# A DLRM tower taken in pairs of units inside a running pipeline, with the last two units cut into parts

## The chip, the cores and the metric

The program runs on one core of one Trainium2 chip. The time is the device time of one execution in microseconds (us); of a kernel that was run several times the median is given. Engines are named as the profile names them: PE is TensorE (PEld its weight loads), DVE is VectorE, ACT is ScalarE, POOL is GpSimd, SP is SyncE, which here only issues DMAs.

## The reference

512 samples, 16 embedding tables of width 256, three compressed-interaction layers, and a small MLP tower.

```python
e = stack([tbl_f[ids[:, f]] for f in range(16)], axis=1)        # 512 x 16 x 256
xk = e
for i in range(3):
    z = einsum('bfe,bge->bfge', e, xk).reshape(B, 256, 256)
    z = relu(einsum('bcl,oc->bol', swapaxes(z, 1, 2), Ws[i]) + bs[i][None, :, None])
    z = sum(z, axis=-1)                                         # 512 x 16
    outs.append(z)
    xk = broadcast_to(z[:, :, None], (B, F, E))
h = concatenate([outs, dense_ctx], axis=1)                      # 512 x 64
h = maximum(h @ W_top1 + b_top1, 0)                             # 64 -> 512
h = maximum(h @ W_top2 + b_top2, 0)                             # 512 -> 256
y = h @ W_top3                                                  # 256 -> 1
```

Everything is float32. The first layer needs all pair products of the 16 features. In layers 2 and 3 `xk` is constant along E, so one layer is a 16x16 table of outer products per sample, a bias and ReLU, and a sum.

## The kernel before

**Units and steps.** The batch is cut into NU = 16 units of 32 samples. A unit passes through the engines over several steps, and step n works on several units at once:

- POOL gathers unit n+2 with four indirect DMAs (`gather`), and forms part of unit n's pair products (`multiply`, `pool_rows(n)` of the 8 rows of the largest rectangle: 4 in most steps, 0 in step 0, 6 in steps 14 and 15).
- PE transposes unit n+1 (`transpose`, into PSUM tile `T`), contracts the products of unit n-1 with the first layer's weights in two halves (`contract`, into `Y`), spreads z over rows for stage n-2 (`spread_rows`, into `ZB`), and projects unit n for layers 2 and 3 (`layer_u`, into `YD`).
- ACT copies `T` to `XT` (`fill`), squares (`square`), copies `YD` to `U` (`read_u`), sums layer 1 (`sum_y`), and sums the outer products of stage n-2, eight blocks of 256 with bias, ReLU and an accumulator (`sum_prod`).
- DVE forms the rest of the pair products (`products`), masks z (`spread_z`, into `zx`) and forms the outer products of stage n-2 (`outer`, into `prod`). A stage s has up to two halves (s, 0) and (s, 1): layer 2 of unit s and layer 3 of unit s-1.

Each engine runs its own fixed list of instructions, in the order of the program text. Semaphores tie the lists together; nothing is reordered by a planner. A wait on an engine holds up all that stands behind it on that engine.

**The tower** runs over three chunks of units, (0, 6), (6, 12), (12, 16). For each chunk PE first moves the sums into rows of `H` by small matmuls with `sel_sb` (`select`), then runs hidden layer 1 (4 matmuls), hidden layer 2 (8 matmuls) and the output (2 matmuls). `MLP_STEPS` places chunk 0 in steps 11 to 15, after the transposes and ahead of `layer_u`; chunks 1 and 2 stand mostly behind the last step. A float32 matmul is two passes on PE, each with its own weight load, and the profile counts the passes.

**The tail** handles stages 14, 15 and 16 after the last contraction. DVE and ACT share its sums (`TAIL_SHARE`), DVE takes over some of the tower's evacuations (`DVE_PIECES`), and stage 16's z goes to `Y` (`zb_last`).

**Unit 0** has all its products on DVE; `dve_products` is raised once, after both halves, so `contract(0, ., 0)` waits for the whole unit. PE transposes units 0 and 1 first, then projects unit 0, then contracts it.

## Time and profile before

| | us |
|---|---|
| median of 3 runs | 172.34 (171.52 to 172.9) |
| the profiled execution | 171.46 |
| its span in the trace | 169.6 |
| PE busy | 137.1 (81%) |
| DVE busy | 144.9 (85%) |
| ACT busy | 126.3 (74%) |
| POOL busy | 121.0 (71%) |

The span is the profiled execution's time without 1.86 us around it. The profiled execution is 0.5% under the median. Busy shares are averages over a filling phase, a regular phase of equal steps (about 30 to 130 us) and a tail (about 140 us to the end); each phase has its own limit.

### The profile page before, as it was taken

What the parts mean: (1) busy time and instruction counts of PE and PEld (TensorE: products, weight loads), DVE (VectorE), ACT (ScalarE), POOL (GpSimd) and SP (SyncE); (2) the same over time, 40 slices, a digit from 0 to 9 for tenths busy, and PEclk for the clock granted to TensorE, in tenths of its full rate; (3) what the DMA queues carried; (4) which work ended last, traced back from release to release, by engine and by line L of the source; (5) the groups of instructions that cost most, each with busy time, mean ns of one, the idle gap of its engine ahead of it and who ended that gap; (6) DMA issues with size and microseconds to landing.
All of it is one profiled execution on the core that took longest, in us unless ns stands there. A gap on an engine that the chain in (4) does not pass through costs nothing.

```text
span 169.6 us, 6453 instructions
## 1 busy us (share of the span) xinstructions
PE 137.1 (81%) x2728; PEld 92.4 (54%) x2728; DVE 144.9 (85%) x136; ACT 126.3 (74%) x441; POOL 121.0 (71%) x84
## 2 busy tenths in 40 slices
PE   0045998988887878787879797999898999993995
PEld 0024665746464646464646464757474876763963
DVE  3169986999999999999999999999999998198330
ACT  3020465586979797979797979798999998977461
POOL 1777989898888888888888888989797995000000
PEclk9999999999999999999999999999999999999599
DMA  2343653131313030303030303031313100000000
GB/s 56 94 123 97 190 151 97 30 98 37 93 33 95 25 101 12 112 9 117 2 114 10 103 20 103 24 99 35 96 32 97 31 4 4 6 0 2 4 0 0
DMA packets 5273, 9.98 MB, mean 59 GB/s; under 512 B 2179, under 2 KB 2947, under 8 KB 5252
## 3 DMA queue, kind: packets, MB, share of 16 engines
q0 software_dynamic: 3072, 8.39, 17.2%
q1 hardware_dynamic: 2036, 1.29, 2.8%
q8 instruction: 14, 0.23, 0.6%
q14 instruction: 7, 0.06, 0.1%
q10 hardware_dynamic: 144, 0.00, 0.0%
HBM read 9.68 MB, written 0.00 MB: 57 GB/s over the span
## 4 chain that ended last, share of the span: by engine, by line
PE 46%; DVE 19%; ACT 18%; issue 8%; POOL 4%; DMA 3%; DVEq 1%; ACTq 0%
PE Y L627 25%; DVE PR L311 13%; ACT prod L387 8%; ACT XT L357 7%; PE T L592 5%; POOL X L329 4%; PE T L688 4%; PE ZB L648 4%; DVE prod L503 3%; PE Y L633 2%; ACT Y L378 2%; PE YD L670 2%; DMA X<-in_table,idx 2%; PE YD L688 2%; PE YD L604 1%
## 5 line engine op out<-in xcount | busy, mean ns | idle before, releaser
L311 DVE TENSOR_TENSOR PR<-T,XT 128x1024 f32<-128x1024 f32 (+2 forms) x72 | 101.1, 1450 | 7.0 <-ACT XT L357 6.9
L627 PE MATMUL Y<-PR,w_sb 128*32 128x272 f32 x1024 | 66.0, 399 | 13.0 <-DVE PR L311 12.6
L329 POOL DMA_INDIRECT X<-in_table,idx x64 | 61.2, 956 | 20.7 <-issue 16.1
L387 ACT ACTIVATE prod<-prod,bias_sb 128x256 f32<-128x256 f32 x122 | 60.1, 498 | 4.2 <-DVE prod L503 4.2
L311 POOL TENSOR_TENSOR PR<-XT 128x2048 f32<-128x2048 f32 (+2 forms) x16 | 59.7, 3734 | 0.3
L627 PEld LDWEIGHTS Y<-PR,w_sb 128*32 128x32 f32 x1024 | 31.1, 110 | 35.7 <-issue 12.1
L503 DVE TENSOR_TENSOR prod<-U,ZB 128x2048 f32<-128x2048 f32 (+1 forms) x18 | 35.6, 1982 | 3.4 <-PE ZB L648 3.3
L378 ACT ACTIVATE Y<-Y,bias 128x136 f32<-128x136 f32 x64 | 21.5, 336 | 14.2 <-PE Y L633 14.2
L592 PE MATMUL T<-ident_sb,X 128*128 128x128 f32 x128 | 21.7, 314 | 12.3 <-DMA X<-in_table,idx 12.3
L357 ACT ACTIVATE XT<-T 128x1024 f32<-128x1024 f32 (+1 forms) x17 | 16.6, 974 | 18.1 <-PE T L592 13.2
L592 PEld LDWEIGHTS T<-ident_sb,X 128*128 128x128 f32 x128 | 17.5, 211 | 14.0 <-issue 9.9
L387 ACT ACTIVATION_READ_ACCUMULATOR prod<-prod,bias_sb 128x1 f32 x122 | 23.3, 191 | 0.0
L363 ACT ACTIVATE PR<-XT 128x1024 f32<-128x1024 f32 x16 | 16.9, 1057 | 0.0
L378 ACT ACTIVATION_READ_ACCUMULATOR Y<-Y,bias 128x1 f32 x64 | 12.7, 198 | 0.0
L633 PEld LDWEIGHTS Y<-minus_half,b0row_sb 1*32 1x32 f32 x256 | 4.9, 102 | 14.0 <-issue 14.0
L604 PE MATMUL YD<-XT,w1l_sb 128*32 128x64 f32 x512 | 11.1, 228 | 0.0
L604 PE MATMUL YD<-XT,w2l_sb 128*32 128x64 f32 x512 | 10.7, 225 | 0.0
L604 PEld LDWEIGHTS YD<-XT,w1l_sb 128*32 128x32 f32 x512 | 8.4, 113 | 2.2 <-issue 1.0
L648 PE MATMUL ZB<-zx,spread_sb 128*128 128x128 f32 (+1 forms) x32 | 7.7, 322 | 2.2 <-DVE zx L489 2.2
L604 PEld LDWEIGHTS YD<-XT,w2l_sb 128*32 128x32 f32 x512 | 8.9, 114 | 0.0
L633 PE MATMUL Y<-minus_half,b0row_sb 1*32 1x32 f32 x256 | 8.4, 202 | 0.0
L648 PEld LDWEIGHTS ZB<-zx,spread_sb 128*128 128x128 f32 x32 | 4.8, 188 | 3.7 <-issue 2.0
(48 smaller groups left out, 69.3 us busy)
## 6 DMA issues: line engine op xcount, KB each, us to landing
X<-in_table,idx POOLq DMA_INDIRECT x64, 2.8
w_sb<-in_w SPq DMA_DIRECT2D x1, 512.0 KB
w_sb<-in_w SPq DMA_DIRECT2D x1, 224.0 KB
sel_sb<-in_sel SPq DMA_DIRECT2D x1, 128.0 KB
ident_sb<-in_ident SPq DMA_DIRECT2D x1, 64.0 KB, 2.1
w1l_sb<-in_w1l SPq DMA_DIRECT2D x1, 64.0 KB
w2l_sb<-in_w2l SPq DMA_DIRECT2D x1, 64.0 KB
w_sb<-in_w SPq DMA_DIRECT2D x1, 64.0 KB
```

Of the source, the lines that this page charges most:

```text
L311: return eng.tensor_tensor(pr, x0.broadcast_to(shape), x1.broadcast_to(shape), ALU.mult)
L329: pool.indirect_dma_start(out=X[:, n % NV, g, :], out_offset=None, in_=table, in_offset=bass.IndirectOffsetOnAxis(ap=idx[:, NT * n + g:NT ...
L357: act.activation(x, t, ACT.Copy).then_inc(xt_ready, len(qs))
L363: act.activation(pr[:, :, PAIRS:COLS], x.rearrange("q (n f) -> q n f", f=F), ACT.Square, scale=ROOT_HALF).then_inc(squared, 1)
L378: last = act.activation(y, y, ACT.Relu, bias=bias2[:], scale=2.0, accum_out=zz[:, n, k:k + 1])
L387: last = act.activation(q, q, ACT.Relu, bias=bias_sb[:, l + 1:l + 2], accum_out=to)
L503: dve.tensor_tensor(prod[:, s % 2, b0:b1, :, :], stage_u(s)[:, b0:b1, :].rearrange("q b (f x) -> q b f x", x=1) .broadcast_to([P, nb, F, F ...
L592: last = pe.transpose(T[:, v, h, c, :], X[:, v, 2 * h:2 * h + 2, :].rearrange("q g (e c) -> q c (g e)", c=NC) [:, c, :], ident_sb[:])
L604: last = pe.matmul(YD[TR * j:TR * j + TR, SB * F * l:SB * F * (l + 1)], w[:, c, :], XT[:, v, :, c, CB * F * j:CB * F * (j + 1)], start=c = ...
L627: pe.matmul(Y[TR * j:TR * j + TR, h, 0:YC], w0_sb[:, c, :], PR[:, v, h, c, CB * j:CB * (j + 1), :].rearrange("q b s -> q (b s)"), start=c ...
L633: last = pe.matmul(out_d[:, :, PAIRS:COLS], b0row_sb[:], minus_half[:].rearrange("q (b f) -> q b f", b=CB), start=False, stop=True)
L648: pe.matmul(zb_of[:, b0:b1, :], spread_sb[:], zx[:, b0:b1, :], start=True, stop=True)\
```

## The change

1. **Start.** Unit 0's products are handed over by halves. PE contracts half 0 before it transposes the second half of unit 1, and half 1 after `layer_u` of unit 0. `keep_busy` puts 10, 8 and 4 matmuls without use of their results between the first waits.
2. **Tower in pairs.** The chunks are (0, 2), (2, 4), (4, 6), (6, 8), (8, 10), (10, 12), (12, 16). From step 5 on, every odd-numbered step of the unit counter selects chunk k and runs hidden layer 2 of chunk k-1; the step after it runs the output of chunk k-1 and hidden layer 1 of chunk k. They stand where `tower_step` stood, between the transposes and `layer_u`, and the loop of steps now covers 7 to 14. `h1` is read by one activation instead of four; the first bias is a row of `w1_sb`.
3. **Copies.** The sums of a pair are first copied by SP, with three DMAs in SBUF, into `pair`, from which PE selects. SP waits for the ACT sums of half (2k+2, 1) and for the previous select.
4. **Last two units.** Stages 14 and 15 are spread and multiplied in parts (`PIECES`), and their spreads stand inside `contract`; `prod` has three buffers instead of two; POOL takes 4 rows in step 14 and 8 in step 15. `layer_u` of unit 15 is done layer by layer.
5. **Folds.** Halves (13, 1) and (14, 1) are folded by POOL from 256 to 64 columns and summed by one DVE reduction each.

The core of the diff (`...` marks what is left out):

```diff
-POOL_ROWS = {0: 0, NU - 2: 6, NU - 1: 6}
-LOOP = range(3, 11)
-CHUNKS = [(0, 6), (6, 12), (12, 16)]
+POOL_ROWS = {0: 0, NU - 1: 8}
+ACT_SHARE = {(NU - 2, 0): 2, (NU - 1, 1): 2, (NU, 1): 2, (NU - 3, 1): 0, (NU - 2, 1): 0}
+FOLDS = [(NU - 3, 1), (NU - 2, 1)]
+PIECES = [(NU - 2, 0), (NU - 2, 1), (NU - 1, 0), (NU - 1, 1), (NU, None)]
+PIECE_BLOCKS = [(0, SB), (SB, 2 * SB), (0, CB), (CB, 2 * SB), (SB, 2 * SB)]
+CHUNKS = [(0, 2), (2, 4), (4, 6), (6, 8), (8, 10), (10, 12), (12, 16)]
+FIRST = 5
+PW = 2 * UB
+LOOP = range(FIRST + 2, NU - 1)
...
+            for k in range(LAST - 1):
+                sp.wait_ge(z0_ready, 2 * CHUNKS[k][1])
+                wait_sums(sp, (CHUNKS[k][1], 1))
+                wait(sp, selected, k)
+                for l, src in enumerate(sums_of(*CHUNKS[k])):
+                    sp.dma_start(pair[:, l, :, :], src).then_inc(paired, 16)
...
+                pool.tensor_tensor(q[:, :, 0:P], q[:, :, 0:P], q[:, :, P:2 * P], ALU.add)\
+                    .then_inc(pool_step, 1)
...
+            def tower_select(n, k):
+                pe.wait_ge(u_read, n)
...
+                if first >= 1:
+                    pe.wait_ge(h1_ready, k)
+                if not isinstance(k, int) or in_flow(k):
+                    pe.wait_ge(paired, 16 * 3 * (k + 1))
+                    select_chunk(selected_psum(0), [pair[:, l, :, :] for l in range(3)])
+                if first >= 1:
+                    for c in range(HC2):
+                        second_hidden(k - 1, c)
+            def tower_hidden(n, k):
+                pe.wait_ge(u_read, n)
+                pe.wait_ge(h_ready, k + 1)
+                wait(pe, h2_ready, HC2 * k)
+                if not isinstance(k, int) or k >= 1:
+                    outputs(k - 1)
+                first_hidden(k, ...)
...
             transpose(0, 0, 0)
+            keep_busy(ZB[:, 2 * P:3 * P], 8)
             pe.wait_ge(consts_in, 16 * 5)
             pe.wait_ge(minus_half_ready, 1)
-            transpose(1, 1, 0)
+            pe.matmul(mask_g_ps, ...).then_inc(mask_ready, 1)
+            transpose(1, 1, 0, (0,))
+            keep_busy(ZB[:, 2 * P:3 * P], 4)
+            contract(0, 0, 0)
+            transpose(1, 1, 0, (1,))
+            layer_u(0, 0)
+            contract(0, 0, 1)
+            transpose(2, 0, 1)
+            layer_u(1, 1)
...
+            with nc.tensor.Fori(1, len(LOOP) // NV + 1) as i:
+                n = NV * i + FIRST
+                step(n, 1, i + FIRST // NV)
+                tower_select(n, i)
+                layer_u(n, 1)
+                step(n + 1, 0, i + FIRST // NV + 1)
+                tower_hidden(n + 1, i)
+                layer_u(n + 1, 0)
```

What PE runs in one pair of regular steps, before (the body of its loop, two steps; `T` transposes, `Y` the contractions, `ZB` the spread, `YD<-XT` the projection `layer_u`):

```order
L627 MATMUL Y<-PR,w_sb 32x272 x16
L633 MATMUL Y<-minus_half,b0row_sb 32x2x16 x4
L592 MATMUL T<-ident_sb,X 128x128 x8
L599 ISA
L604 MATMUL YD<-XT,w1l_sb 32x64 x16
L604 MATMUL YD<-XT,w2l_sb 32x64 x16
```

Now, from the transposes of the select step to its projection, and the same place of the step after it:

```order
L693 MATMUL T<-ident_sb,X 128x128 x8
L793 ISA
L751 MATMUL YD<-pair,sel_sb 32x4x2 x24
L772 MATMUL YD<-h,w_sb 128x64 x8
L700 REGISTER_ALU
L706 MATMUL YD<-XT,w1l_sb 32x64 x16
```

```order
L693 MATMUL T<-ident_sb,X 128x128 x8
L779 MATMUL YD<-h,w_sb 1x64 x2
L765 ISA
L765 MATMUL YD<-H,w_sb 128x64 x4
L700 REGISTER_ALU
L706 MATMUL YD<-XT,w1l_sb 32x64 x16
```

Each pair of steps has gained 24 small and 14 tower matmuls; before, steps 3 to 10 held none of them. The end of PE's list, before, behind the last contraction:

```order
L684 MATMUL T<-H,w_sb 128x192 x4
L648 MATMUL ZB<-zx,spread_sb 128x128
L670 MATMUL YD<-zz,sel_sb 32x8x2 x8
L670 MATMUL YD<-zz,sel_sb 32x6x2 x8
L670 MATMUL YD<-z,sel_sb 32x4x2 x8
L688 MATMUL T<-h,w_sb 128x192 x4
L648 MATMUL Y<-zx,spread_sb 128x64
L688 MATMUL T<-h,w_sb 128x192 x4
```

and now:

```order
L706 MATMUL T<-XT,w2l_sb 32x64 x16
L743 MATMUL ZB<-zx,spread_sb 128x96
L772 MATMUL YD<-h,w_sb 128x64 x8
L743 MATMUL T<-zx,spread_sb 128x64
L751 MATMUL YD<-zz,sel_sb 32x4x2 x16
L751 MATMUL YD<-z,sel_sb 32x4x2 x8
```

The spread of stage 16 (128x64) stood behind a hidden layer of 192 columns; it now stands behind one of 64.

## Rows read from the trace of the kernel before

**Rows 1.** Busy time of each engine in two stretches (us, count), then PE's clock, DMA.

```profile
80.00:90.00 10.00, 8.50 (x183) 5.38 (x186) 10.00 (x7) 9.05 (x33) 8.90 (x6) 1.00 0.22 66
...
150.00:160.00 10.00, 7.06 (x71) 6.53 (x72) 6.35 (x16) 6.95 (x28) 0.00 (x0) 0.85 0.01 2
```

**Rows 2.** Timeline, DVE, one regular step: start, duration, what, count, [idle before <- releaser].

```profile
79.13 0.27 DVE L489 TENSOR_TENSOR zx<-zz,ZB 128x128 f32<-128x128 f32 x1
...
87.65 0.28 DVE L489 TENSOR_TENSOR zx<-zz,ZB 128x128 f32<-128x128 f32 x1
```

**Rows 3.** Timeline, PE, one regular step and the start of the next.

```profile
85.88 2.04 PE L627 MATMUL Y<-PR,w_sb 128*32 128x272 f32 x32 [1.50 <-DVE PR L311]
...
90.63 1.23 PE L592 MATMUL T<-ident_sb,X 128*128 128x128 f32 x8
...
91.80 0.65 PE L604 MATMUL YD<-XT,w1l_sb 128*32 128x64 f32 x32
...
92.27 0.63 PE L604 MATMUL YD<-XT,w2l_sb 128*32 128x64 f32 x32
```

**Rows 4.** Timeline, PE: loads under 16 columns; step 11 with select; unit 15's transposes.

```profile
21.87 0.30 PEld L709 LDWEIGHTS ZB<-mask_g_sb,ident_sb 128*128 128x128 f32 x2
...
107.60 1.23 PE L592 MATMUL T<-ident_sb,X 128*128 128x128 f32 x8
...
109.98 0.25 PE L604 MATMUL YD<-XT,w1l_sb 128*32 128x64 f32 x2
...
132.94 1.23 PE L592 MATMUL T<-ident_sb,X 128*128 128x128 f32 x8
```

**Rows 5.** Timeline, ACT, the same regular step.

```profile
83.43 1.02 ACT L357 ACTIVATE XT<-T 128x1024 f32<-128x1024 f32 x1 [0.36 <-issue]
...
84.35 0.50 ACT L387 ACTIVATE prod<-prod,bias_sb 128x256 f32<-128x256 f32 x1
...
88.28 0.26 ACT L369 ACTIVATE U<-YD 128x128 f32<-128x128 f32 x1
...
90.77 0.35 ACT L378 ACTIVATE Y<-Y,bias 128x136 f32<-128x136 f32 x1 [0.57 <-PE Y L633]
```

**Rows 6.** DMA issues: what, queue, kind, count, size, median us from issue to landing.

```profile
X<-in_table,idx POOLq DMA_INDIRECT x64, 2.8
...
bias_sb<-in_bias SPq DMA_DIRECT2D x1, 1.5 KB, 1.8
```

**Rows 7.** Timeline, SP's issue of a DMA, and POOL around its last gather.

```profile
1.66 0.42 SPq L283 DMA_DIRECT2D bias_sb<-in_bias  x1
...
130.18 0.94 POOL L329 DMA_INDIRECT X<-in_table,idx  x1 [0.30 <-issue]
131.14 8.38 POOL L311 TENSOR_TENSOR PR<-XT 128x3072 f32<-128x3072 f32 x2
```

**Rows 8.** Timeline, the start: DVE's and PE's first work, DVE's second wait.

```profile
9.96 14.73 DVE L311 TENSOR_TENSOR PR<-T,XT 128x1024 f32<-128x1024 f32 x12 [4.82 <-ACT XT L357]
...
18.96 2.79 PE L627 MATMUL Y<-PR,w_sb 128*32 128x272 f32 x32 [0.37 <-ACT PR L363]
...
26.81 2.29 DVE L311 TENSOR_TENSOR PR<-T,XT 128x2048 f32<-128x2048 f32 x1 [2.11 <-ACT XT L357]
```

**Rows 9.** Timeline, the tail, from the last contraction to the last activation.

```profile
149.73 0.26 PE L633 MATMUL Y<-minus_half,b0row_sb 1*32 1x32 f32 x8
...
154.93 0.22 DVE L489 TENSOR_TENSOR zx<-zz,ZB 128x64 f32<-128x64 f32 x1
...
156.53 2.44 PE L688 MATMUL T<-h,w_sb 128*128 128x192 f32 x8
...
158.77 0.53 PE L648 MATMUL Y<-zx,spread_sb 128*128 128x64 f32 x2
...
159.53 1.22 DVE L503 TENSOR_TENSOR prod<-U,Y 128x1024 f32<-128x1024 f32 x1 [3.21 <-PE Y L648]
...
167.71 0.27 ACT L395 ACTIVATE y_sb<-Y 1x128 f32<-1x128 f32 x1 [1.35 <-PE Y L693]
```

More of the change, by code:

```diff
@@ L19 @@
 NV = 2
+NPR = 3
 EH = 64
@@ L697, in _, with select_chunk, first_hidden @@
-            pe.wait_ge(ident_in, 16)
+            def select_chunk(to, layers):
+                for l, src in enumerate(layers):
+                    last = select(to, l, src)
+                last.then_inc(selected, 1)
+            def first_hidden(k, cols):
+                w = 0 if not isinstance(k, int) else k
+                per = HC1 // len(hidden1_psum(w))
+                for c in range(HC1):
+                    pe.matmul(hidden1_psum(w)[c // per][:, c % per, :], w1_sb[:, c * P:(c + 1) * P],
+                              H[:, cols], start=True, stop=True).then_inc(hidden1, 1)
@@ new lines, in second_hidden, with outputs @@
+            def second_hidden(k, c):
+                w = 0 if not isinstance(k, int) else k
+                for q in range(HC1):
+                    last = pe.matmul(hidden2_psum(w, c), w2_sb[:, q, c * P:(c + 1) * P], h1_of(w, q),
+                                     start=q == 0, stop=q == HC1 - 1)
+                last.then_inc(hidden2, 1)
+            def outputs(k):
+                w = 0 if not isinstance(k, int) else k
+                for q in range(HC2):
+                    last = pe.matmul(output_psum(w), w3_sb[:, q:q + 1], h2_of(w, q), start=q == 0,
+                                     stop=q == HC2 - 1)
+                last.then_inc(output, 1)
@@ L698, in _, with step @@
+            pe.wait_ge(ident_in, 16)
+            keep_busy(ZB[:, 2 * P:3 * P], 10)
+            def step(n, v, r):
+                first = n if isinstance(n, int) else LOOP[0]
+                contract(n - 1, 1 - v, 0)
+                if first == 2:
+                    pe.wait_ge(spread_in, 16)
+                spread_rows(n - 2)
+                contract(n - 1, 1 - v, 1)
+                transpose(n + 1, 1 - v, r + v)
             transpose(0, 0, 0)
+            keep_busy(ZB[:, 2 * P:3 * P], 8)
@@ L736, in _ @@
-            contract(NU - 1, last, 1)
-            for done in MLP_STEPS[NU - 1]:
-                wait_sbuf(pe, done)
-            pe.wait_ge(u_read, NU)
-            for c in range(HC1):
-                tower((1, HIDDEN1, c))
-            spread_rows(NU - 1)
-            n0 = CHUNKS[2][0]
-            select(2, 0, n0, NU)
-            select(2, 1, n0, NU - 1)
-            select(2, 2, n0, NU - 2)
-            tower((1, HIDDEN2, 0))
-            spread_rows(NU)
-            tower((1, HIDDEN2, 1))
@@ new lines, in _ @@
+            last = (NU - 1) % NV
+            layer_u(NU - 1, last, (0,))
+            contract(NU - 2, 1 - last, 0)
+            spread_rows(NU - 3)
+            contract(NU - 2, 1 - last, 1)
+            contract(NU - 1, last, 0, [(NU - 2, 0)])
+            contract(NU - 1, last, 1, [(NU - 2, 1), (NU - 1, 0)])
+            layer_u(NU - 1, last, (1,))
+            spread_rows(NU - 1, 1)
+            pe.wait_ge(h1_ready, LAST - 1)
+            for c in range(HC2):
+                second_hidden(LAST - 2, c)
@@ new lines, in _ @@
+            select(to, 1, zz[:, n0 + 1:n1 + 1, SB:2 * SB])
+            for half in STAGES:
+                if half[1] == 1 and half[0] > n0:
+                    wait_sums(pe, half)
+            select(to, 2, z2[:, n0:n1, :]).then_inc(selected, 1)
+            pe.wait_ge(h1_ready, LAST)
+            pe.wait_ge(y_done, LAST - 1)
+            second_hidden(LAST - 1, 0)
+            pe.wait_ge(h_ready, LAST + 1)
+            first_hidden(LAST, samples(LAST))
+            second_hidden(LAST - 1, 1)
```

614 lines of the change are left out of this document (332 added, 282 removed).

## The prediction

> **What bounds the kernel now.** I read the busy time by stretch first, then the timeline of one regular step, then the start and the tail. In a regular step DVE has no idle time at all (10.00 of 10, [rows 1]), and the same z mask returns after 87.65 - 79.13 = 8.52 us [rows 2]. So from about 30 to 130 us DVE sets the pace. PE is close behind: from the first contraction to the projection it needs 91.80 - 85.88 = 5.92 us, the projection's two groups start 0.47 apart and so take about 0.94, together 6.86 of 8.52, with 1.66 free, of which 1.50 shows as idle time ahead of the contraction [rows 3]. ACT waits 0.36 and 0.57 in a step [rows 5]. POOL has its own chain, gathers and products without a gap: its last gather is issued at 130.18, and a gather lands 2.8 after its issue [rows 6, 7]. The tail is a chain through all engines from the end of the last contraction, 149.73 + 0.26 = 150.0 [rows 9], to the span's end at 169.6. In it stage 16's z is masked at 154.93, but its spread runs only at 158.77, because PE is in a hidden layer until then, and DVE waits 3.21 for it [rows 9].
>
> **The start.** DVE's first 14.73 us of products end at 24.69; then it waits 2.11 us for unit 2 [rows 8]. The cause is PE: it cannot contract unit 0 before 18.96, when both halves are done, and transposes unit 2 after that. With halves, half 0 can be contracted near 14, and unit 2 is transposed by about 22, ahead of DVE's need at 24.7. Gain 2.1. This needs PE at its upper clock level: one contraction half took 2.79 at 18.96 against 2.04 later [rows 3, 8]. If `keep_busy` did nothing for the clock, its 8 and 4 matmuls would stand ahead of the contraction and eat up to all of the 2.1. I take 2.1 and keep 0 as the other end.
>
> **The regular steps.** Select: in step 11 the way from transposes to projection is 109.98 - 107.60 = 2.38 [rows 4] against 91.80 - 90.63 = 1.17 without it [rows 3], so 24 small matmuls cost 1.21. Hidden layers on 64 columns: no row shows them. Two passes under only 16 columns have their weight loads 0.11 apart (0.30 for two of 0.19 each, [rows 4]), so a pass does not get cheaper than 0.11 with few columns. Hidden 2 is 16 passes, 1.76; hidden 1 is 8 passes, 0.88; the output's four passes load one column, about 0.2. In the order of PE's list a pair of steps is then 2 x 6.86 + 1.21 + 1.76 + 0.88 + 0.2 = 17.8 us, against DVE's 2 x 8.52 = 17.04. **PE becomes the bound of the loop, by 0.7 a pair.** With passes at 0.05, half that, it would be 16.4 and PE would stay hidden; at 0.15 it would be 18.7. I take 0.11, since it is the one row with few columns and full weights.
>
> The new copies close a longer ring. From the start of a select on: select and hidden 2 2.97, projection 0.94, contractions and transposes of the hidden step 90.63 + 1.23 - 85.88 = 5.98 [rows 3], 0.1 to ACT, `fill` until its sums start 84.35 - 83.43 = 0.92, eight sums 88.28 - 84.35 = 3.93 [rows 5], 0.1; then SP issues three DMAs at 0.42 and a little each [rows 7], so the last starts 0.95 later and lands. Landing: 1.8 us for a small table from DRAM, 2.8 for a gather [rows 6]; I take 2.2, nearer to the small table, since each copy is many runs of 16 bytes. Then the next select can start. The ring is 2.97 + 0.94 + 5.98 + 0.1 + 0.92 + 3.93 + 0.1 + 0.95 + 2.2 = **18.1 us a pair**, 1.1 over DVE. At the ends of 1.8 and 2.8 it is 17.7 (then PE's 17.8 decides) and 18.7. The loop has four pairs. In the first the transposes of the hidden step are late by 2.97 - 1.66 = 1.3; the other three add 1.1 each: the last transposes, unit 15's, come 4.5 late against the old pace. ACT's extra reads (three short ones, or one long and one short, together about 0.5 a step) are paid by its 0.93 of waits [rows 5].
>
> The Trainium skill's page "DMA: Bandwidth & Descriptors", section "Anatomy of one DMA — SWDGE (gpsimd) path", gives about 2.0 us fixed per DMA, most of it the write receipt. By it the ring would be an estimated 17.9, and the time about 0.8 less than below; no row here shows a copy within SBUF.
>
> **Unit 15 and the last contractions.** Unit 15 was transposed from 132.94 to 134.2 [rows 4], 0.3 ahead of the old pace (90.63 + 5 x 8.52 = 133.2), since POOL took 6 rows in step 14. Now: 134.2 + 0.3 - 2.1 + 4.5 = 136.9. Behind it PE has output and hidden 1 (1.1), the projections (0.94 + 0.47 = 1.4), and four contraction halves with four spreads. Two halves with one spread took 90.63 - 85.88 = 4.75 [rows 3], of which I give the spread 0.43; so 9.5 + 0.9 = 10.4. 136.9 + 1.1 + 1.4 + 10.4 = 149.8, where it was 150.0. The waits in front of them are met: POOL's products of unit 15 are 4096 elements at 8.38 / 4608 = 1.82 ns [rows 7], 7.4 us from about 138, so 145.4, before the last half needs them.
>
> **The tail.** From the last contraction: layer 1 sums 0.8, mask and spread 0.8, outer product in two parts 1.2, its last two sums by ACT, mask, spread of stage 16 by about +4.5; DVE meanwhile finishes (15, 1) at +5.1, outer (16, 1) 1.2, fold 0.3, two sums 1.0: +7.7. Then select 0.5, its read 0.3, half of a hidden 2 left in the way 0.9, hidden 1 0.9, the other half 0.9, hidden 2 1.8, read 0.4, output 0.5, read 0.3: +14.2 with a few hand-overs; minus what ACT and PE overlap, +13.8; the store 169.6 - 167.98 = 1.6. The tail is 15.4 us long where it was 19.6, so 4.2 shorter; the 3.21 of DVE's wait [rows 9] is most of it. The folds by POOL (1024, 512 and 256 elements at 1.82 ns, 3.3 us) end before DVE comes to them.
>
> **Sum.** 149.8 + 15.4 = 165.2 for the span, 4.4 less than 169.6. Against the profiled execution, 171.46, this is 167.1; this execution is 0.9 under the median of 172.34, and of that I add about 0.3: **167.4**.
>
> **The rivals.**
>
> (1) The ring does not bind: the passes are cheap or the copies land early enough. Then POOL decides: last gather 130.18 + 2.8 = 133.0, its half transposed by 133.6 instead of 136.9. 3.3 less: 164.1. For it: select waits only 0.1 in the first pair, so small errors decide. Against: PE alone is at 17.8, above 17.04. Chance 0.24.
>
> (2) The clock. PE falls to its lower level in gaps: in the stretch from 150 to 160 the granted clock averaged 0.85 [rows 1], and the hidden half of 156.53 to 158.97 lies in it [rows 9]. Such a fall in the new tail, or a start without the upper level, costs 1.5 to 2.1: 169. Chance 0.14.
>
> (3) GpSimd in DVE's way. Before, POOL is finished when DVE sums in SBUF; now its folds run beside DVE's sums of (14, 0) and delay them by at most one fold instruction, 1024 x 1.82 ns = 1.9 us, on the way to stage 15: 169.1. For it speaks nothing in the rows, against it that DVE's products run beside POOL's in every regular step at full speed, though those read one side from PSUM. The Trainium skill, page "SBUF — State Buffer", section "Who interferes with whom", says that the two share a port pair as an exclusive lock, and it would give this delay if DVE's sums take both ports. Chance 0.08.
>
> (4) Slower: **the copies land late.** Place: PE's wait ahead of each select in the loop, with projection, contractions and transposes queued behind it, and so ACT and DVE. Every us of landing over 2.2 comes back four times. Equal to before at 2.2 + 4.9 / 4 = 3.4 us; slower by 1% from 2.2 + 6.6 / 4 = 3.9. At 3.9 the time is 167.4 + 6.7 = 174.1. For it: many tiny packets on engines that gather at the same time; against: 1.8 to 2.8 for all DMAs seen. Chance 0.16, of which 0.10 beyond 1%.
>
> The forecast itself has 0.38.
>
> **Numbers.** About 1% is what a measurement of this kernel can tell from no change. Below 170.6: the forecast 0.35 of its 0.38 (landing at 2.8 gives 169.8), rival 1 0.24, rival 2 0.10, rival 3 0.07: 0.76. Within 1%: 0.03 + 0.04 + 0.01 + 0.06 = 0.14. Slower by over 1%: 0.10. The range goes from rival 1 with 0.8 off its time for a better tail, 163.3, to the forecast with landing at 2.8 and one fall of the clock, 171.6; it leaves out most of rival 4 and little below.
>
> **What would show it.** After the change, in the loop: the z mask returns every 9.0 to 9.1 us on average instead of 8.52, DVE idles about 0.5 a step ahead of the products that need XT, and PE waits for the copies ahead of the select; hidden 2 on 64 columns has 0.11 from load to load. At the start DVE's 2.11 wait is gone, and the contraction near 14 takes about 2.0. Unit 15's transposes end near 136.9, the last contraction near 149.8, and no wait of DVE over 1 us stands ahead of stage 16's outer product. If the pace stays 8.52, rival 1 holds and my PE sum is wrong; if the wait ahead of the select is over 1.5 us a pair, rival 4 does; if DVE's sums of (14, 0) are stretched by the length of a fold, rival 3.

## The result and the profile after

The changed kernel takes **183.53 us** (median of 4 runs, 181.82 to 184.59) against 172.31 (171.52 to 172.9) for the kernel before on the same chip: ratio 1.0631, 95% interval 1.0579 to 1.0682. It is slower, and outside the range of 163.3 to 171.6. The profiled execution took 181.82, its span is 180.0, 10.4 more than 169.6. Throughout, medians are over all runs of a kernel, and ratios leave out the runs that took over 1.5% longer than its fastest.

| point of the program | before | forecast | after |
|---|---|---|---|
| z mask of the first full step | 36.52 | 34.4 | 36.23 |
| z mask of stage 13 (now the last one in one piece) | 138.18 | - | 146.87 |
| unit 15's transposes end | 134.2 | 136.9 | 143.7 |
| last contraction ends | 150.0 | 149.8 | 157.0 |
| span ends | 169.6 | 165.2 | 180.0 |

Of the 10.4 us, 7.0 are there when the last contraction ends, and 3.4 come in the tail behind it.

Busy time by stretch, the kernel after (columns as in [rows 1]):

```profile
80.00:90.00 10.00, 9.51 (x191) 6.23 (x184) 9.35 (x7) 7.97 (x31) 8.91 (x6) 1.00 0.24 67
130.00:140.00 10.00, 10.00 (x197) 7.63 (x190) 7.73 (x6) 6.98 (x26) 6.22 (x4) 0.83 0.22 53
150.00:160.00 10.00, 9.36 (x162) 5.47 (x153) 8.13 (x17) 8.40 (x34) 8.96 (x5) 1.00 0.02 4
160.00:170.00 10.00, 8.80 (x122) 8.15 (x121) 4.71 (x13) 4.58 (x20) 1.10 (x2) 0.63 0.01 2
170.00:180.00 10.00, 7.74 (x42) 7.11 (x41) 0.84 (x3) 1.81 (x7) 0.00 (x0) 0.67 0.00 0
```

Against [rows 1] the roles are exchanged: DVE, 10.00 of 10 before, now stands still for 0.65, and PE is nearly full. From 72 to 142, the loop, PE is busy 68.47 of 70. TensorE has two clock levels here, 1.2 and 2.4 GHz. The 0.63 and 0.67 of the last two stretches are means over both, with the lower one for about two thirds of the time or more (an estimate from these means).

**One pair of steps**, timeline, PE, which answers to [rows 3] and [rows 4]:

```profile
87.64 2.04 PE L721 MATMUL Y<-PR,w_sb 128*32 128x272 f32 x32 [0.49 <-issue]
...
92.39 1.23 PE L693 MATMUL T<-ident_sb,X 128*128 128x128 f32 x8
93.55 1.49 PE L751 MATMUL YD<-pair,sel_sb 128*32 128x8 f32 x48
94.96 2.00 PE L772 MATMUL YD<-h,w_sb 128*128 128x64 f32 x16
96.89 0.65 PE L706 MATMUL YD<-XT,w1l_sb 128*32 128x64 f32 x32
...
97.89 2.04 PE L721 MATMUL Y<-PR,w_sb 128*32 128x272 f32 x32
...
102.63 1.23 PE L693 MATMUL T<-ident_sb,X 128*128 128x128 f32 x8
103.79 0.38 PE L779 MATMUL YD<-h,w_sb 128*1 128x64 f32 x4
104.11 1.10 PE L765 MATMUL YD<-H,w_sb 113*128 x8
105.14 0.65 PE L706 MATMUL YD<-XT,w1l_sb 128*32 128x64 f32 x32
...
106.61 2.04 PE L721 MATMUL Y<-PR,w_sb 128*32 128x272 f32 x32 [0.37 <-issue]
```

From contraction to contraction of the next pair it is 106.61 - 87.64 = 18.97 us, and nothing in it waits for another engine. The distances between starts give each piece: select 94.96 - 93.55 = 1.41, hidden layer 2 96.89 - 94.96 = 1.93 (0.12 a pass), output 0.32, hidden layer 1 105.14 - 104.11 = 1.03, and from the start of the second step's projection to the next contraction 106.61 - 105.14 = 1.47, where the same way in the first step is 97.89 - 96.89 = 1.00. The 0.37 and 0.49 marked "issue" stand at the place where the loop of instructions returns. PE hardly waits for the copies: from 72 to 142 it does so once, 0.30 at 112.89.

**The start**, timelines of PE, DVE and POOL, the kernel after. The last row is POOL's last gather of unit 3; of the kernel before the same row reads 26.50.

```profile
29.58 0.75 PE L693 MATMUL T<-ident_sb,X 128*128 128x128 f32 x4
32.06 0.75 PE L693 MATMUL T<-ident_sb,X 128*128 128x128 f32 x4 [1.74 <-DMA X<-in_table,idx]
32.74 1.07 PE L706 MATMUL YD<-XT,w1l_sb 128*32 128x64 f32 x32
...
34.42 2.90 PE L721 MATMUL Y<-PR,w_sb 128*32 128x272 f32 x32
```

```profile
26.72 0.21 DVE L580 TENSOR_TENSOR zx<-zz,ZB 128x64 f32<-128x64 f32 x1
...
34.02 2.29 DVE L329 TENSOR_TENSOR PR<-T,XT 128x2048 f32<-128x2048 f32 x1 [2.03 <-ACT XT L394]
36.23 0.28 DVE L580 TENSOR_TENSOR zx<-zz,ZB 128x128 f32<-128x128 f32 x1
```

```profile
26.68 0.95 POOL L347 DMA_INDIRECT X<-in_table,idx  x1 [0.30 <-issue]
```

DVE's wait of 2.11 for unit 2 [rows 8] is gone, and the first z mask comes 2.3 earlier. Then PE is early for unit 3 as well, and unit 3 is not there. Its last gather was issued at 26.68, no earlier than before, since POOL's chain has no gap, and it landed 5.3 us after its issue, where the same gather took 3.2 before and the median of all is 2.8. PE waits 1.74, DVE 2.03. In the same place the projection takes 1.07 instead of 0.65: the clock has fallen. The next mask is 0.3 earlier than before. The late landing isn't the new start's doing: in experiment 12, with the old start, the same gather takes 5.3 too, and in experiment 1, with the new start alone, 2.8. What makes it late was not tried.

**The tail.** Stage 16's outer product now follows DVE's sums without a wait, where [rows 9] had 3.21. But PE comes late. Its timeline from hidden layer 1 of the last but one chunk on:

```profile
164.22 1.97 PE L765 MATMUL T<-H,w_sb 113*128 113x64 f32 x8
166.12 1.54 PE L751 MATMUL YD<-zz,sel_sb 128*32 128x16 f32 x29
...
168.42 1.97 PE L772 MATMUL T<-h,w_sb 128*128 128x64 f32 x8
170.19 2.02 PE L765 MATMUL Y<-H,w_sb 113*128 113x128 f32 x8
172.00 1.81 PE L772 MATMUL T<-h,w_sb 128*128 128x64 f32 x8
173.60 3.23 PE L896 MATMUL T<-h,w_sb 128*128 128x128 f32 x16
```

The eight passes at 164.22 took 1.10 at 104.11 in the loop. Here they take 1.97: it is the lower level of the clock, and it lasts nearly to the end. DVE's last sum ends at 164.8. What follows, 15.2 us, is PE's list, the reads between its layers and the store.

### The profile page after: what moved, and what is told of

Read it like the earlier page. It is cut to its first block, busy times and chain, and to the rows that moved or that the text cites. A ratio compares the mean times of both kernels' runs of the same rounds, so it can differ in the third digit from the quotient of the medians.

```text
span 180.0 us, 7141 instructions
## 1 busy us (share of the span) xinstructions
PE 162.9 (90%) x3048; PEld 118.3 (66%) x3048; DVE 145.3 (81%) x138; ACT 125.5 (70%) x444; POOL 129.4 (72%) x89
## 4 chain that ended last, share of the span: by engine, by line
PE 58%; ACT 9%; DVE 3%; issue 2%; DMA 1%; SPq 1%; DVEq 0%
PE Y L721 24%; PE YD L751 5%; PE T L693 5%; ACT prod L433 5%; PE YD L706 5%; PE YD L772 4%; PE ZB L743 3%; DVE PR L329 2%; PE Y L727 2%; ACT XT L394 2%; PE T L772 2%; PE YD L765 2%; PE T L896 2%; DMA pair<-z 1%; ACT Y L421 1%
## 5 line engine op out<-in xcount | busy, mean ns | idle before, releaser
L329 DVE TENSOR_TENSOR PR<-T,XT 128x1024 f32<-128x1024 f32 (+3 forms) x70 | 101.7, 1489 | 8.8 <-ACT XT L394 8.6
L721 PE MATMUL Y<-PR,w_sb 128*32 128x272 f32 x1024 | 67.6, 403 | 5.3 <-DVE PR L329 4.1
L329 POOL TENSOR_TENSOR PR<-XT 128x2048 f32<-128x2048 f32 x16 | 59.7, 3732 | 9.7 <-ACT XT L394 9.4
L433 ACT ACTIVATE prod<-prod,bias_sb 128x256 f32<-128x256 f32 x114 | 56.2, 497 | 0.6 <-DVE prod L596 0.6
L596 DVE TENSOR_TENSOR prod<-U,ZB 128x2048 f32<-128x2048 f32 (+2 forms) x18 | 33.9, 1895 | 7.1 <-PE ZB L743 7.1
L433 ACT ACTIVATION_READ_ACCUMULATOR prod<-prod,bias_sb 128x1 f32 x114 | 21.7, 191 | 0.0
L693 PEld LDWEIGHTS T<-ident_sb,X 128*128 128x128 f32 x128 | 17.1, 210 | 4.5 <-DMA X<-in_table,idx 3.9
L812 PE MATMUL ZB<-ident_sb 128*128 128x128 f32 x44 | 7.6, 345 | 3.6 <-DMA ident_sb<-in_ident 3.6
L772 PE MATMUL YD<-h,w_sb 128*128 128x64 f32 x80 | 9.9, 277 | 0.0
L812 PEld LDWEIGHTS ZB<-ident_sb 128*128 128x128 f32 x44 | 7.2, 256 | 3.6 <-DMA ident_sb<-in_ident 3.6
L772 PEld LDWEIGHTS YD<-h,w_sb 128*128 128x128 f32 x80 | 9.3, 192 | 0.1
```

The source lines that it names most:

```text
L329: return eng.tensor_tensor(pr, x0.broadcast_to(shape), x1.broadcast_to(shape), ALU.mult)
L433: last = act.activation(q, q, ACT.Relu, bias=bias_sb[:, l + 1:l + 2], accum_out=sum_to(half)[:, b:b + 1])
L596: dve.tensor_tensor(prod[:, s % NPR, b0:b1, :, :], stage_u(s)[:, b0:b1, :].rearrange("q b (f x) -> q b f x", x=1) .broadcast_to([P, nb, F, ...
L693: last = pe.transpose(T[:, v, h, c, :], X[:, v, 2 * h:2 * h + 2, :].rearrange("q g (e c) -> q c (g e)", c=NC) [:, c, :], ident_sb[:])
L721: pe.matmul(Y[TR * j:TR * j + TR, h, 0:YC], w0_sb[:, c, :], PR[:, v, h, c, CB * j:CB * (j + 1), :].rearrange("q b s -> q (b s)"), start=c ...
L772: last = pe.matmul(hidden2_psum(w, c), w2_sb[:, q, c * P:(c + 1) * P], h1_of(w, q), start=q == 0, stop=q == HC1 - 1)
```

## The experiments

Three things are to be told apart: what made the loop longer (the copies and their ring, PE's own time for narrow pieces, the return of the loop), what the start is worth, and whether the tail is long by its work or by its clock. Every kernel was timed beside the kernel before on its own chip; the ratios are to that.

**1. The start alone**, put into the kernel before:

```diff
-            transpose(1, 1, 0)
...
+            keep_busy(ZB[:, 2 * P:3 * P], 8)
...
+            transpose(1, 1, 0, (0,))
+            keep_busy(ZB[:, 2 * P:3 * P], 4)
+            contract(0, 0, 0)
+            transpose(1, 1, 0, (1,))
```

> The kernel before with the start of the change alone (unit 0 contracted by halves, the first matmuls that keep PE busy). Theory G, gathers decide: in the trace of the change unit 3's second transposes wait for their gather until 32.06, and the mask that stood at 36.52 before stands at 36.23; so the start gives at most 0.3 us, 172.0, no difference. Rival, as I forecast: 2.1 us are kept to the end, 170.2.

Measured: 174.08 (172.18 to 174.79, 10 runs), ratio 1.0066 (1.002 to 1.0112). The 2.1 us are not in the total; it is no faster. But the mask did not stay at 36.23, as the first theory had it: in the profile (of the slowest run, 174.79) it stands at 35.31, 1.2 earlier than before, and the lead lasts until stage 10 (112.02 for 113.21). Then it melts: PE waits 2.09 for unit 15's gather, and the mask of stage 13 is at 139.61 instead of 138.18.

**2. No copies.** `pair` is a constant, its DMAs are gone, and PE does not wait for them:

```diff
-                    sp.dma_start(pair[:, l, :, :], src).then_inc(paired, 16)
+                    pass
```

> The change without its copies: pair is filled once at the start, SP issues no copy and PE does not wait for one (the selects take constants, so the tower's results for those units are not the reference's; the matmuls are the same). Theory P, PE's own work sets the loop's pace (19.1 us a pair): under 1 us less than 183.5. Rival 4 of the prediction, the copies come late and hold PE up: 4 us or more come back, 179 or less, and the mask returns every 8.9 us or less in the loop.

Measured: 181.55 (181.06 to 185.85), ratio 1.0532 (1.0483 to 1.0582): by the two ratios 1.7 us less than the change, more than the first theory allows and far less than rival 4 needs. The profile is of the slowest run, 185.85, where the other four lie within 0.5 of each other. In it a pair takes longer than with copies. PE:

```profile
98.23 1.08 PE L707 MATMUL YD<-XT,w1l_sb 128*32 128x64 f32 x32
...
99.94 2.84 PE L722 MATMUL Y<-PR,w_sb 128*32 128x272 f32 x32
```

The same slow rows begin at 77.69, 118.71 and 139.19 too: in each of the four pairs the clock falls behind hidden layer 2, and a pair is 20.5. Of that the fall is (99.94 - 98.23) - 1.00 for the projections and 2.84 - 2.04 for the contraction, 1.5, so 19.0 without it, as with the copies. So the copies are not what makes a pair 19 us long. By the totals some 1.7 of the change's 11 us may be theirs (an estimate, 0.4 to 3.0 by the two intervals). From 70 to 150 the granted clock averages 0.91, although PE waits for nobody from 69 on until these rows. The other four runs cannot have had all four falls, since 4 x 1.5 is more than what separates them from this one.

**3. Light pairs.** The copies stay; in the loop, select is 3 matmuls instead of 24 and hidden layer 2 is 2 instead of 8:

```diff
-                    select_chunk(selected_psum(0), [pair[:, l, :, :] for l in range(3)])
+                    select_chunk(selected_psum(0), [pair[:, l, :, :] for l in range(3)], light=True)
...
-                        second_hidden(k - 1, c)
+                        second_hidden(k - 1, c, light=True)
```

> The change with the tower's matmuls in the loop cut: a select is 3 matmuls instead of 24, hidden layer 2 is 2 instead of 8 (so the tower's results for those units are not the reference's), all waits and copies kept. Theory P: PE has 2.6 us less per pair, 19.1 becomes about 16.5, DVE's 17.04 sets the pace again; from step 9 on the mask returns every 8.5 to 8.6 us and the time falls by 7 to 9 us, to about 175. Rival 4, the copies: the ring loses the same 2.6 us only in part, since copies still come after ACT's sums; 2 to 4 us less, 180, with PE waiting for the copies ahead of each select.

Measured: 174.15 (172.99 to 174.97), ratio 1.0128 (1.0072 to 1.0184). PE, one select step:

```profile
91.03 1.23 PE L693 MATMUL T<-ident_sb,X 128*128 128x128 f32 x8
92.19 0.31 PE L759 MATMUL YD<-ident_sb,sel_sb 128*32 128x64 f32 x6
92.43 0.66 PE L778 MATMUL YD<-h,w_sb 128*128 128x64 f32 x4
93.02 0.65 PE L706 MATMUL YD<-XT,w1l_sb 128*32 128x64 f32 x32
...
94.35 2.04 PE L721 MATMUL Y<-PR,w_sb 128*32 128x272 f32 x32 [0.23 <-DVE PR L329]
```

The wait is back where [rows 3] had it: PE waits for DVE again, and the masks return every 8.52 up to 130.37. The mask of stage 13 is at 138.42 instead of 146.87. So with the return of the loop and with the copies, but without 2.5 us of PE's work a pair, the loop costs nothing. The 8.4 us come from PE's time for the tower, together with the one fall of the clock that this work had in the change (1.5). The tail is still long (32.8 us from that mask to the end), with a clock of 0.68 from 150 to 160 and 0.64 behind it.

**4. Short matmuls in the tail**, whose results nobody reads, 3 ahead of stage 15's last spread and 5 ahead of stage 16's:

```diff
+            keep_busy(T_bank[1][1][:, 0:P], 3)
             spread_rows(NU - 1, 1)
...
+            keep_busy(T_bank[1][1][:, 0:P], 5)
             spread_rows(NU)
```

> The change with 3 and 5 matmuls of 128 columns without use put into PE's two idle places of the tail (ahead of the spreads of stages 15 and 16; PE stood idle there for 0.65 and 1.12 us). Theory I, PE's clock falls at 162 because PE stood idle: the clock stays at its upper level in the tail and the time falls by 5 to 6 us, to 178. Theory D, it falls because the work there is weight loads with few columns under them (it also fell at 135, inside 14 us in which PE had no idle time at all): no change, 183.5, or a later fall and 1 to 2 us less.

Measured: 174.53, 177.81, 183.11 and 182.66. The runs spread over 8.6 us, so there is no ratio: the mean clock was 0.99 and 0.98 in the first two and 0.94 and 0.95 in the others. The profiled one is the fastest, clock 1.00 from 150 on, and it shows the tail's work at the upper level: 172.7 - 155.6 = 17.1 from the end of the last contraction, against 180.0 - 157.0 = 23.0. None of its four pairs has a fall of the clock: from the mask of stage 5 to that of stage 13 it takes 145.50 - 70.70 = 74.80, against 76.56 in the change and 4 x 17.04 = 68.16 at the old pace. So 6.6 of the loop's 8.4 us are there without any fall.

**5. The loop written out**, so that nothing returns:

```diff
-            with nc.tensor.Fori(1, len(LOOP) // NV + 1) as i:
+            for i in range(1, len(LOOP) // NV + 1):
```

> The change with PE's loop over steps 7 to 14 written out (same instructions, no branch back). In the trace of the change PE starts the contraction behind each branch back 0.65 us after its last weight load with nothing to wait for, where it needs none elsewhere. Theory P: three branches back and the exit, 0.65 us each, come back whole, since PE sets the pace: 2 to 2.6 us less, 181. Rival: the branch only fills time in which DVE's products are not ready anyway: no change, 183.5.

Measured: 189.55 (187.77 to 191.01), ratio 1.1001 (1.0907 to 1.1095). No theory had this. PE's timeline:

```profile
89.61 2.08 PE L721 MATMUL Y<-PR,w_sb 128*32 128x272 f32 x32
...
97.14 2.31 PE L772 MATMUL YD<-h,w_sb 128*128 128x64 f32 x16
99.38 1.08 PE L706 MATMUL YD<-XT,w1l_sb 128*32 128x64 f32 x32
...
117.01 1.46 PE L751 MATMUL YD<-pair,sel_sb 128*32 128x8 f32 x48 [1.31 <-DMA pair<-z]
```

The gap is gone as intended (the contraction at 89.61 starts 0.44 behind the second projection's start at 89.17). What comes in its place is a fall of the clock behind hidden layer 2 at 99, waits for the copies (1.31 here, 2.5 in all), and behind it another fall that lasts: from 120 to 130 PE is busy 10.00 of 10 at a granted clock of 0.70. The removed gap was cheaper than what it let in. Why this fall is longer than the others stays open.

**6. One move in the kernel before.** Half of a hidden layer and stage 16's spread are put ahead of a select that waits for sums (it had waited 2.58 us there, and they behind it):

```diff
-            select(2, 2, n0, NU - 2)
             tower((1, HIDDEN2, 0))
             spread_rows(NU)
+            select(2, 2, n0, NU - 2)
```

> The kernel before with one move in PE's tail: the first half of chunk 1's hidden layer 2 and the spread of stage 16 now stand ahead of the last but one select. DVE's wait of 3.21 us for that spread is in the chain of the tail: with the spread at about 155.3 instead of 158.8, 2.5 to 3.5 us less, 169.2. Rival: the time goes into the next wait, the sums of stage 16 behind ACT's list and the hidden layers that still stand in front of the last chunk: under 1 us less, 171.5.

Measured: **168.68** (168.65 to 168.87), ratio 0.9821 (0.9792 to 0.9851), faster than both kernels. The spread, at 158.77 in [rows 9]:

```profile
154.90 0.43 PE L648 MATMUL Y<-zx,spread_sb 128*128 128x64 f32 x2 [0.35 <-DVE zx L489]
```

It runs as soon as its z is masked. The clock is 1.00 from 150 to 160, where [rows 1] have 0.85. The hidden half that took 2.44 at 156.53 [rows 9] takes 1.57 here, so 0.9 of the gain is the clock. The tail's rebuilding was forecast to bring 4.2 us; this move brings 3.2. Its tail, from the last contraction's end, is 166.9 - 149.7 = 17.2 us, as long as the rebuilt one at the upper level (17.1).

**7. Hidden layer 2 over 128 columns** in the steps of the changed kernel, 64 of them zeros:

```diff
-                    last = pe.matmul(hidden2_psum(w, c), w2_sb[:, q, c * P:(c + 1) * P], h1_of(w, q),
+                    last = pe.matmul(at, w2_sb[:, q, c * P:(c + 1) * P],
+                                     h1[:, 0 if in_flow(w) else w - LAST + 2, q, :],
```

> The change with hidden layer 2 of every pair run over 128 columns instead of 64 (the upper 64 hold earlier or zero values and their results are not read). Same number of passes. Theory P: a pass is as long as its weight load, 0.12 us, with 64 as with 128 columns, so the loop's pace stays at 19.1 us a pair. Theory D, thin work lowers the clock: with twice the columns the clock does not fall at 135 and falls later or not at all in the tail, 2 to 6 us less, 178 to 181. Rival: a pass costs by its columns: 0.9 us more a pair or more, 187.

Measured: 178.62 (178.35 to 179.23), ratio 1.0391 (1.0359 to 1.0423). PE:

```profile
94.88 1.49 PE L752 MATMUL YD<-pair,sel_sb 128*32 128x8 f32 x48
96.29 2.05 PE L775 MATMUL YD<-h,w_sb 128*128 128x128 f32 x16
98.27 0.65 PE L707 MATMUL YD<-XT,w1l_sb 128*32 128x64 f32 x32
```

Twice the columns cost 98.27 - 96.29 = 1.98 instead of 1.93. So a pass costs the same with 64 as with 128 columns, which fits a pass bound by the load of its 128 x 128 weights. It does not go on: with 192 columns the layer took 2.70 in the kernel before.

```profile
134.01 2.77 PE L688 MATMUL YD<-h,w_sb 128*128 128x192 f32 x16
```

The Trainium skill, page "TensorE: Matmul & The Clock Gate", section "LDWEIGHTS (loading the stationary operand)", has a load take the number of columns of the weights over 1.2 GHz, an estimated 0.107 us; the trace agrees within 0.02 (0.12 a pass). And the useless columns made the kernel some 4 us faster than the change (by the two ratios). The clock is 1.00 over all of 72 to 142, 0.71 from 160 to 170 and 0.87 behind it, where the change has 0.98, 0.63 and 0.67. In the profiles the gain is in the tail, 177.4 - 157.3 = 20.1 for 23.0. The loop ends no earlier, with the mask of stage 13 at 147.18: it has no fall, but PE waits 0.67 for a gather and 0.19 and 0.65 for copies.

**8. Chunks of four units.** Chunks (0, 4), (4, 8), (8, 12), (12, 16); a chunk's tower is spread over four steps, straight from the sums, without copies. Steps 7 to 14 are written out, so PE's loop does not return in them, and 6 short matmuls stand ahead of the last spread:

```diff
-CHUNKS = [(0, 2), (2, 4), (4, 6), (6, 8), (8, 10), (10, 12), (12, 16)]
-FIRST = 5
-PW = 2 * UB
+CHUNKS = [(0, 4), (4, 8), (8, 12), (12, 16)]
+FIRST = 7
+PW = 4 * UB
+SPAN = 4
...
+            keep_busy(T_bank[1][1][:, 0:P], 6)
```

> The change with the tower in chunks of four units, (0, 4), (4, 8), (8, 12), (12, 16), one phase in each step from step 7 on, selected straight from the sums without copies, steps 7 to 14 without a loop, and 6 matmuls without use ahead of the spread of stage 16 where the hidden layer of 64 columns stood. Theory P: the weight loads of the tower are halved, a step's tower part is 1.9 us at most against 1.66 free, so DVE sets the pace and the last mask of the loop is back at about 138.2; the tail as in the run in which the clock held, 27 us behind it: 167 to 169 if the clock holds, 171 to 173 if it falls. Rival: the tail's gain was tied to the pairs being done early: 172 or more in any case.

Measured: 171.47 (168.39 to 173.99), ratio 0.9846 (0.9782 to 0.991). This kernel overwrites part of one chunk's hidden layer 2, so it counts for its time alone; the next one doesn't.

**9. The same, with hidden layer 2 in a place of its own**, and no other edit:

```diff
-                return YD[:, P + w * (c + 1):P + w * (c + 2)]
+                return YD[:, P + w * c:P + w * (c + 1)]
```

> The change with the steps' tower in chunks of four units instead of pairs, taken from the sums without copies, and six short matmuls that nobody reads ahead of unit 15's spread. Theory P (TensorE's own time for the tower in narrow pieces is what the loop lost): the passes over the weights come half as often, the distance of two z masks is back at 8.5 us up to unit 14, and the time is 168 to 172. Rival C (a chunk's width doesn't matter, the tower inside the steps does): the masks stay at 9.5 a step and the time is 180 or more.

Measured: 168.29, 167.53, 172.82 and 172.98, without a ratio for their spread. The masks return every 8.52 up to 122.39. The first theory's pace holds, the second falls. Four things differ from the change at once, though: width, spreading over four steps, no copies, no return of the loop. Experiment 3 kept the copies and the return and was back at 8.52 as well, so the last two are not needed for it. Width and spreading were not told apart. The change's tower takes 1.41 + 1.93 + 0.32 + 1.03 = 4.7 us in a pair of steps that has 2 x 1.66 = 3.3 free, however it is spread within the pair.

**10. Fours with the old start:**

```diff
-            keep_busy(ZB[:, 2 * P:3 * P], 10)
...
-            keep_busy(ZB[:, 2 * P:3 * P], 8)
...
-            transpose(1, 1, 0, (0,))
-            keep_busy(ZB[:, 2 * P:3 * P], 4)
-            contract(0, 0, 0)
-            transpose(1, 1, 0, (1,))
+            transpose(1, 1, 0)
             layer_u(0, 0)
+            contract(0, 0, 0)
```

> The same kernel in fours with the start of the kernel before (unit 1 filled in one piece, unit 0 contracted after it, no short matmuls there). Theory S (the 2.1 us won at the start are given back at unit 3's gather, and the wait there lowers TensorE's clock): the time is that of the kernel in fours or up to 2 lower, and the granted clock between 30 and 40 us is 1.00. Rival (the start is worth what it showed at unit 2): it is 2 us slower.

Measured: 169.25 (168.12 to 172.63), ratio 0.9787 (0.9697 to 0.9877). Clock 1.00 from 30 to 40. It isn't slower than with the new start, though runs that spread over 4 to 5 us cannot tell 2. The masks say more: the first full one is at 36.23 here and at 37.18 in 9, that of stage 13 at 138.52 and 139.10. PE in a step with hidden layer 2:

```profile
99.86 1.95 PE L771 MATMUL YD<-h,w_sb 128*128 128x128 f32 x16
101.74 0.65 PE L705 MATMUL YD<-XT,w1l_sb 128*32 128x64 f32 x32
```

The layer costs 1.88 as for a pair, but once for four units, and it is one step's only tower work, next to 1.66 us that PE has free in it.

**11. The changed kernel with 128 columns and the tail's short matmuls together** (the edits of 7 and 4):

> The change with its second layer's matmuls in the steps over 128 columns instead of 64 (the other 64 are zeros) and 3 and 5 matmuls of 128 columns that nobody reads ahead of the spreads of units 14 and 15. Theory T (what the tail lost is TensorE's clock, and it falls where TensorE's work is narrow or stands still): the clock stays at 1.00 from 150 on, and the time is 173 to 176, steadily. Rival (the tail's work itself is long): 178 to 180, as with the 128 columns alone.

Measured: 177.25 (176.17 to 179.16), ratio 1.0298 (1.0181 to 1.0415). More than expected in the median, 176.2 in the profiled run, and not steady: two runs lie at 176.2 with a mean clock of 0.99, the others at 178.3 and 179.2 with 0.97. In the profiled one the clock is 1.00 from 20 to 170, and the tail:

```profile
164.00 1.10 PE L766 MATMUL T<-H,w_sb 113*128 113x64 f32 x8 [0.19 <-ACT H L446]
165.04 0.99 PE L752 MATMUL YD<-zz,sel_sb 128*32 128x16 f32 x29
...
169.24 1.95 PE L902 MATMUL T<-h,w_sb 128*128 128x128 f32 x16
```

1.10 for 1.97, 1.95 for 3.23. From the last contraction's end to the end it is again 174.4 - 157.3 = 17.1. Even so the kernel is slower than before: the loop is as long as ever, with the mask of stage 13 at 147.15. That it ends there at a clock of 1.00 throughout shows that the clock is not what makes the loop long. (It waits 0.8 in all for copies in the loop and 0.8 once for a gather, which is why it ends no earlier than the change's with its one fall.)

**12. The change with the old start** (the edit of 10, in pairs):

> The change with the start of the kernel before; the loop in pairs and the spread tail stay. Theory S (the start's gain is given back at unit 3's gather): within 1 us of the change, or up to 2 lower where the clock stays at 1.00 between 30 and 40 us. Rival (the start is worth 2 us to the end): 185.5.

Measured: 184.21 (182.07 to 188.44), ratio 1.0703 (1.0589 to 1.0818). The fastest run, 182.07, is within 0.3 of the change's 181.82. The interval is too wide to tell half a us; that the start is not worth 2 us the profile shows: with the old one the second mask comes at 36.65 instead of 36.23, and that of stage 13 at 147.01 instead of 146.87. In the loop each kernel has one fall of the clock up to there.

**13. Fours, the old start, and more short matmuls** where PE stood still in the tail:

```diff
+            keep_busy(T_bank[1][1][:, 0:P], 3)
             spread_rows(NU - 1, 1)
-            keep_busy(T_bank[1][1][:, 0:P], 6)
+            keep_busy(T_bank[1][1][:, 0:P], 10)
             spread_rows(NU)
```

> The kernel in fours with the old start and more short matmuls that nobody reads where TensorE stood still in its tail: 3 ahead of unit 15's first spread (it waited 0.64 us there) and 10 instead of 6 ahead of the last spread (1.52). Theory T (the tail's clock follows TensorE's stands there): the clock stays at 1.00 from 150 on and all runs lie at 167 to 168.5. Rival (the clock falls whatever stands there, by the chip's state): the runs spread as before, from 168 to 173.

Measured: **168.33** (168.08 to 168.75), ratio 0.9776 (0.971 to 0.9843). PE:

```profile
150.34 2.42 PE L813 MATMUL T<-ident_sb 128*128 128x128 f32 x20
153.39 0.44 PE L742 MATMUL T<-zx,spread_sb 128*128 128x64 f32 x2 [0.63 <-DVE zx L579]
```

The stand of 1.52 us ahead of the last spread has shrunk to 0.63, the clock is 1.00 from 149 to 166, and the four runs lie within 0.7, where those of 9 and 10 spread over 5.4 and 4.5. That favours the first theory and doesn't prove it: these are four runs on another chip than those of 9 and 10. With 6's one move it is the fastest of all, and no measurement here tells the two apart.

## Why the prediction was wrong, step by step

The span was forecast at 165.2 and came to 180.0, 14.8 more: 1.8 at the start, 3.8 in the loop's masks, 1.2 from there to unit 15's transposes, 0.4 from those to the last contraction, 7.6 in the tail.

**The start: gain 2.1, measured 0.3.** The mechanism held up to unit 2: the contraction at 14.72 took 2.04, the upper level, and DVE's wait vanished. The step that failed is that the gain was carried to the end. It passed over the next late thing, POOL's gathers: unit 3's in the change, which on top of that landed 2.1 us later after its issue than before, and in experiment 1, where the masks were 1.2 earlier for most of the loop, unit 15's. I had written POOL's chain down as one without a gap; that sentence already said that nothing can come earlier than POOL lets it. In the total the start brought nothing in 1; in 10 and 12 the mask of stage 13 moved by 0.6 the other way and by 0.1.

**The loop: PE 17.8 a pair, the ring 18.1, measured 18.97.** That PE becomes the bound was right, and 3 shows it; the sum was short by 1.2, term for term: select 1.41 for 1.21, hidden layer 2 1.93 for 1.76, hidden layer 1 1.03 for 0.88, output 0.32 for 0.2, and 2.47 for the two projections instead of 1.88. The first rests on a row that I read wrongly: 1.21 was the extra time of a step in which the projection's weights mixed with the end of select. Those of the layers rest on 0.11 for a pass, from a load under 16 columns, when it is 0.12 to 0.13. The last has the loop's return, 0.37 to 0.49, for which I had no term: before, PE waited for DVE at that very place [rows 3], and the return lay hidden in the wait. The pairs measured by their masks are 17.88, 19.09, 19.36 and 20.23; the last holds a fall of the clock. Over 17.04 that is 8.4 against the forecast's 4.6 (1.3 + 3 x 1.1; it went on with 4.5). Some 1.5 of the difference is the fall, the rest the sum. The error is small in each row, but where PE is the bound every 0.1 us counts four times.

**The ring of copies: 18.1, measured 19.3, and still not the cause.** I had it 0.3 longer than PE's own work, and that is how it came out: both grew. From the select at 93.55 to the one at 112.89, which waited 0.30 for its copies, it is 19.34 us. Select and hidden layer 2 are 3.34 of it where I had 2.97; the last copy is issued 110.27 - 108.97 = 1.30 behind the first, where I had 0.95, since SP takes 0.62 for each; and from that issue to the select it is 2.62, where I had 2.2. In the other pairs the copies were there in time. Experiment 2 shows that without them a pair still is 19.0. Where PE's own work got shorter or other waits moved it, they did hold PE up: 2.5 us in 5, 0.8 in 7 and 11. Rival 4 (chance 0.16) needed a landing of over 3.9 and a wait of over 1.5 a pair; the kernel did get slower, for another reason. Rival 1 is out as well: the pace never was 8.52 in the loop.

**The fall of the clock: rival 2, right in kind, wrong in size.** I had it at 1.5 to 2.1 us and a chance of 0.14. In the tail alone it cost 23.0 - 17.1 = 5.9, for it did not fall in one gap but stayed down over nearly all of PE's last 15 us. I had counted one hidden layer at the lower level, as in [rows 9]. The right reading was that the new tail is almost wholly PE's work on few columns, which takes 1.6 to 1.8 times as long if the clock is down (3.23 for 1.95, 1.97 for 1.10). The profiled runs of 4, 11 and 13 show it from the other side.

**The tail: 15.4, measured 23.0, at the upper level 17.1.** DVE's part came as forecast: it ends 164.8 - 157.0 = 7.8 behind the last contraction, where I had 7.7. PE's part was short by 1.7. The largest piece is the last chunk's select: I gave it 0.5, as if only its last layer were left. PE is in hidden layer 1 of the chunk before until then and takes all 48 passes behind it, from 165.04 to 166.46 in 11, 1.42 us.

**The folds on POOL: hidden, though slower than I had them.** The first took 3.70 us for 1024 elements, not 1.9:

```profile
152.35 3.70 POOL L373 TENSOR_SCALAR prod<-prod,bias_sb 128x1024 f32<-128x1024 f32 x1
156.14 1.28 POOL L379 TENSOR_TENSOR prod<-prod 128x512 f32<-128x512 f32 x1
```

```profile
156.60 0.53 DVE L608 TENSOR_SCALAR_CACHE_REDUCE prod<-prod,floor_sb,lifted_sb 128x256 f32<-128x256 f32 x1
...
161.42 0.53 DVE L608 TENSOR_SCALAR_CACHE_REDUCE prod<-prod,floor_sb,lifted_sb 128x256 f32<-128x256 f32 x1
```

POOL had finished when DVE came to its reductions, and DVE's sum at 156.60, beside a fold, takes 0.53 like the one at 161.42, beside none. The longest fold, 3.70, ran beside none of DVE's sums, and the product beside it, at 153.25, took its usual 1.22. So nothing of rival 3 shows. The Trainium skill, page "SBUF — State Buffer", section "Who interferes with whom", leaves out of the shared lock the scalar form that also writes its accumulator, and these sums are of that form: on the one beside a fold, the trace agrees. I had cited the rule without that exception.

## What to carry to other kernels

Work moved beside an engine that sets the pace is free only up to the idle time of the engine that takes it. Count that idle time first (here 1.66 us a step, in a step that was given 3.3), with every matmul pass at its weight load. A tower in chunks of two units loads the same weights twice as often as one in fours. In twos it asked for 4.7 us in a pair of steps with 3.3 free, and the loop grew by 8.4; in fours, spread over four steps, it grew by nothing (how much of that is the width and how much the spreading was not told apart). And before a stage is rebuilt, look for the one instruction that stands in front of another one's wait: the move of 6 alone brought as much as the best kernel in fours.
